# The front of a deformable-convolution stage: weights as 128 rows, positions as a tenth tap, tap 8 selected from the parts, another first item in the ring of PSUM banks

## The chip, the core and the metric

The kernel runs on one core of one Trainium2 chip. The metric is the device time of one execution in microseconds (us). PE is the matmul engine (TensorE), ACT evaluates functions and evicts PSUM (ScalarE), DVE is VectorE, POOL is GpSimd, SP issues most DMAs (SyncE). Engines run their own instruction streams and wait for each other on semaphores. Matmuls here are float32, and each one appears in the trace as two passes.

## The reference

Five stages follow each other on x of shape (8, 32, 16, 16); the change lies in the first, and the other four (a convolution with Fourier attention, Nystrom attention, two mixtures of layers with data-dependent routing) stay as they are.

```python
x = x + deform(groupnorm(x), w_off, b_off, w_dcn)     # groups of one channel
# deform: KK = 9 taps, 18 offset channels (dy, dx per tap)
offset = conv3x3(x, w_off) + b_off
y  = row - 1 + ky + dy ;  xc = col - 1 + kx + dx       # sampling position
sampled[c, k, n] = bilinear(x[c], y[k, n], xc[k, n])   # zero outside
out[o, n] = sum_{c, k} sampled[c, k, n] * w_dcn[o, c, k]
```

## The kernel before

The data lies as 128 partitions: 4 images (`bi`) times 32 channels, with two groups (`g`) of 256 pixels in the free dimension, so one tile is 128x512. DVE normalizes x into `xnp` (with a border) and `xn` (semaphore `xn`); ACT gives the square root in between (`var`, `std`).

The offset convolution is 36 matmuls of 32x32 (line 539): per image one bank `ps[0..3]`, and in the bank the four 32-row column groups take taps k % 4. The sampling positions (row, column, tap shift and bias, from the four rows of `lineb`) are one matmul into `ps[4]` (line 532) ahead of it. The four banks are evicted to four tiles, the `parts4`: two by ACT (line 1181), two by DVE (line 1464). A matmul with `eye32` adds up the column groups of each part in `ps[4]` (line 565), and ACT evicts the sum as `offC` (line 1194).

A position enters as a hat function of its distance to each grid line. Matmuls with 0/1 weights select the rows of `offC` for each tap: line 572 selects tap 8 of all images into `ps[2]` (`sel8_w`), line 577 taps 0 to 3 of one image each into `ps[3..6]`. ACT takes the absolute distance (line 1189, `distance`), and DVE cuts it to the hat (line 1472, `hat`). Then comes the ring: "items" of four matmuls into four of the banks 0 to 6 in rotation. `expand` (line 632) spreads a hat to the pixel grid for one image, `expand8` (line 640) does so for tap 8 of the four images, and both are squared on the way out: three banks by ACT (`squares`, line 1209), one copied by DVE (line 1500) and squared by POOL (line 427). Weight items (`half_of_weights`, line 550) multiply `xn` with the taps' weights, and ACT and DVE evict them (lines 1185, 1468). The products of the two (line 649) add up in bank 7, which a matmul with zeros opens (line 677). `bank_free` writes the waits for each item's banks by hand, `FILL_ACT`, `FILL_DVE`, `ACT_FILL` and `DVE_FILL` count what each engine has evicted before item 0, and the order of items on each engine is written out.

The loads: SP issues x, `lineb`, two blocks of constants (`cstb`), `parb` and `rowb`; ACT issues the early columns of the weights `w32b` in two DMAs, each broadcast from 32 rows to four copies. SP then waits for both and issues the late loads. `par_in` is one semaphore for `lineb`, `parb` and `rowb`.

Of the kernel before, what the change touches and what calls it, by code (L numbers as in the profile page):

```python
# [20 lines left out]
ACT = mybir.ActivationFunctionType  # L21
# [18 lines left out]
SMALL = 16 * 3  # L40
LATE = 16 * 10

# [3 lines left out]
for _n, _k in (("off", KK * C), ("dcn", KK * C), ("conv", KK * CH), ("qkv", 3 * P), ("gate", EXP), ("ln", 2),  # L46
               ("v", LAYERS * LHEADS * C), ("q", LAYERS * LHEADS * C)):
    W32[_n] = (_at, _at + _k)
    _at += _k
W32_COLS = _at  # L50
W32_OFF, W32_EARLY = W32["off"][1], W32["conv"][1]
# [4 lines left out]
for _n, _k in (("mask4", BI), ("eye32", C), ("negq", 1), ("sel8", 8), ("spread", PT * P), ("gather", PT * 32),  # L56
               ("ident", P), ("flip", P), ("mask8", HEADS),
               ("rep16", P), ("mask16", P), ("swap", P), ("dft", PT * 2 * N)):
    CST[_n] = (_at, _at + _k)
    _at += _k  # L60
CST_COLS = _at
CST_EARLY, CST_MID = CST["sel8"][1], CST["gather"][1]


PAR = ("bn_g", "bn_b", "bn_m", "bn_v", "cg2_w", "cg2_b", "cg1_w", "cg1_b", "cgbn_g", "cgbn_b", "cgbn_m",
       "cgbn_v", "tau", "gate_b")
ROWS = {"b_out": (0, C)}
ROW_COLS = C


LINES = P + BG * N
# [7 lines left out]
    "x_in", "cst_in", "mid_in", "w32_in", "taps_in", "par_in", "late_in",  # L79
# [24 lines left out]
FILL_ACT = {"part": 1, "weights": 3, "sum": 5, "far": 6}  # L104
FILL_DVE = {"part": 1, "weights": 3, "more": 5}
ACT_FILL, DVE_FILL = 10, 8
GROUPS = {1: (1, 2, 3, 4), 2: (8, 9, 11, 12), 3: (14, 15, 16, 17), 4: (18, 19, 20, 21)}
ITEM = {1: (0, 0, 0), 2: (0, 0, 1), 3: (0, 0, 2), 4: (0, 0, 3), 8: (0, 1, 0), 9: (0, 1, 1), 11: (0, 1, 2),
        12: (0, 1, 3), 14: (1, 0, 0), 15: (1, 0, 1), 16: (1, 0, 2), 17: (1, 0, 3), 18: (1, 1, 0), 19: (1, 1, 1),
        20: (1, 1, 2), 21: (1, 1, 3)}  # L110
SQUARED = (0, 1, 2, 3, 4, 7, 8, 9, 11, 12, 14, 15, 16, 17, 18, 19, 20, 21)
FREED = {8: 1, 9: 2, 11: 3, 12: 4, 14: 6, 15: 5, 16: 7, 17: 8, 18: 9, 19: 10, 20: 11, 21: 12}
G_ITEM, SEL_ITEM, GC_ITEM = {5: 0, 6: 1}, 10, 13
ALL_DCN = 18
EX_COUNT = {0: 1, 1: 2, 2: 3, 3: 4, 4: 5, 7: 6, 8: 7, 9: 8, 11: 9, 12: 10, 13: 11, 14: 13, 15: 14, 16: 15, 17: 16,
            18: 17, 19: 18, 20: 19, 21: 20}
# [24 lines left out]
def build(nc, x, cst, w32, par, rows, lines, toep, w_out, moe_w1, moe_w2, moe_b2, am, fm, keys, rec_a, rec_b, out):  # L141
    ctx = ExitStack()
    with ctx:
# [9 lines left out]
        parb = sb("parb", len(PAR))  # L153
        rowb = sb("rowb", ROW_COLS)
# [16 lines left out]
        def row_(n):  # L171
            return rowb[:, ROWS[n][0]:ROWS[n][1]]

# [13 lines left out]
        lineb = sb("lineb", LINES, parts=4)  # L187
# [31 lines left out]
        sel_w, sel8_w = outf, gatef[:, 0:P]  # L219
# [111 lines left out]
        def home(item, j):  # L331


            first = {0: 0, 1: 4, 2: 8, 3: 12, 4: 16, 7: 20, 8: 0, 14: 20}
            if item in first:
                return room[first[item] + j]
            column = {9: (1, 0), 11: (1, 1), 12: (1, 2), 15: (1, 3), 16: (2, 0), 17: (2, 1), 18: (2, 2), 19: (2, 3),
                      20: (3, 0), 21: (3, 1)}[item]
# [6 lines left out]
        def _(sp):  # L345
            sp.dma_start(xC.rearrange("p (g n) -> p g n", g=BG),
                         x.rearrange("(g b) c n -> (b c) g n", g=BG)).then_inc(S["x_in"], 16)
            sp.dma_start(lineb, lines).then_inc(S["par_in"], 16)
            sp.dma_start(cstb[:, 0:CST_EARLY], cst[:, 0:CST_EARLY]).then_inc(S["cst_in"], 16)
            sp.dma_start(cstb[:, CST_EARLY:CST_MID], cst[:, CST_EARLY:CST_MID]).then_inc(S["mid_in"], 16)  # L350
            sp.dma_start(parb, par.unsqueeze(0).to_broadcast([B, CH, len(PAR)])).then_inc(S["par_in"], 16)
            sp.dma_start(rowb, rows.partition_broadcast(P)).then_inc(S["par_in"], 16)
            sp.wait_ge(S["w32_in"], 16)
            sp.wait_ge(S["taps_in"], 16)
            sp.dma_start(cstb[:, CST_MID:CST_COLS], cst[:, CST_MID:CST_COLS]).then_inc(S["late_in"], 16)
            sp.dma_start(w32b[:, W32_EARLY:W32_COLS], w32[:, W32_EARLY:W32_COLS].unsqueeze(0)
# [1622 lines left out]
```

## Time and profile before

| | |
|---|---|
| median of 3 runs | 344.14 us (341.44 to 345.53) |
| the profiled execution | 342.19 us, span 340.2 us |
| mean granted clock of TensorE | 0.948 |
| busy PE, DVE, ACT, POOL | 84%, 48%, 43%, 16% of the span |
| first piece of the product stretch | 35.91 us |
| end of the stage's matmuls | 75.34 us |

Busy shares are means over stages with different limits: the first 36 us are the part to read closely. The span goes from the first to the last instruction; the time includes what lies around it.

### The profile page before, as it was taken

What the parts mean: (1) busy time and instruction counts of PE and PEld (TensorE: products, weight loads), DVE (VectorE), ACT (ScalarE), POOL (GpSimd) and SP (SyncE); (2) the same over time, 40 slices, a digit from 0 to 9 for tenths busy, and PEclk for the clock granted to TensorE, in tenths of its full rate; (3) what the DMA queues carried; (4) which work ended last, traced back from release to release, by engine and by line L of the source; (5) the groups of instructions that cost most, each with busy time, mean ns of one, the idle gap of its engine ahead of it and who ended that gap; (6) DMA issues with size and microseconds to landing.
All of it is one profiled execution on the core that took longest, in us unless ns stands there. A gap on an engine that the chain in (4) does not pass through costs nothing.

```text
span 340.2 us, 5837 instructions
## 1 busy us (share of the span) xinstructions
PE 286.2 (84%) x1954; PEld 168.8 (50%) x1954; DVE 163.4 (48%) x423; ACT 145.5 (43%) x329; POOL 54.1 (16%) x61
## 2 busy tenths in 40 slices
PE   5989999999888999989988789778976787588873
PEld 1333333357335798979953465666422442125521
DVE  3152335823767559787656544113413763126730
ACT  1156786733525634646423301120141692225940
POOL 3104826521006000160000002330000000000001
PEclk9698999999999899999998959999999999879999
DMA  3864200000000000000000000000000000000000
GB/s 100 204 122 100 78 0 4 2 2 0 2 0 1 0 2 0 3 1 0 2 0 0 2 0 0 0 0 3 2 19 17 0 0 0 17 17 0 0 0 31
DMA packets 4193, 6.20 MB, mean 18 GB/s; under 512 B 1318, under 2 KB 3750, under 8 KB 4013
## 3 DMA queue, kind: packets, MB, share of 16 engines
q1 hardware_dynamic: 3910, 5.58, 7.2%
q10 hardware_dynamic: 264, 0.37, 0.3%
q8 instruction: 12, 0.20, 0.3%
q14 instruction: 7, 0.06, 0.1%
HBM read 5.69 MB, written 0.26 MB: 17 GB/s over the span
## 4 chain that ended last, share of the span: by engine, by line
PE 59%; DVE 16%; ACT 7%; issue 7%; DMA 6%; SPq 2%; DVEq 1%; ACTq 0%
PE ps L649 6%; PE ps L632 6%; PE ps L517 5%; DMA recB<-rec_b 4%; PE ps L883 4%; PE ps L889 3%; PE ps L1018 2%; PE ps L871 2%; ACT arena L1383 2%; DMA rowb<-rows 2%; DVE rmax L1845 2%; PE ps L1130 2%; PE ps L539 1%; PE ps L1010 1%; PE ps L823 1%
## 5 line engine op out<-in xcount | busy, mean ns | idle before, releaser
L517 PE MATMUL ps<-xC,cstb 128*128 128x512 f32 x102 | 50.6, 640 | 0.0
L517 PEld LDWEIGHTS ps<-xC,cstb 128*128 128x128 f32 x102 | 20.2, 207 | 25.3 <-issue 25.0
L632 PE MATMUL ps<-arena,cstb 32*128 32x512 f32 x128 | 22.2, 652 | 0.6 <-ACT arena L1189 0.6
L1209 ACT ACTIVATE bds<-ps 128x512 f32<-128x512 f32 x32 | 17.2, 599 | 7.4 <-PE ps L632 6.1
L486 POOL TENSOR_TENSOR arena<-w32b,cstb 128x1024 f32<-128x1024 f32 x4 | 7.6, 1894 | 64.7 <-PEq L1004 50.8
L495 POOL TENSOR_TENSOR ln_a<-tC,hC 128x512 f32<-128x512 f32 x1 | 1.3, 1263 | 104.1 <-DVE hC L1880 104.1
L649 PE MATMUL ps<-bds,arena 128*32 128x256 f32 x160 | 17.4, 384 | 0.0
L883 PE MATMUL ps<-arena 128*128 128x160 f32 x96 | 15.3, 307 | 2.3 <-issue 1.2
L1383 ACT ACTIVATE arena<-ps,rmax 128x256 f32<-128x256 f32 x32 | 14.8, 470 | 5.2 <-DVE rmax L1845 5.2
L883 PEld LDWEIGHTS ps<-arena 128*128 128x128 f32 x96 | 13.3, 190 | 3.4 <-DVE arena L1708 1.9
L1400 ACT ACTIVATE arena<-ps,w2c 128x512 f32<-128x512 f32 x16 | 9.7, 688 | 11.2 <-PE ps L1130 11.2
L1100 PE MATMUL ps<-cstb,arena 128*128 128x128 f32 x64 | 10.5, 286 | 4.3 <-DVE arena L1853 4.2
L1137 PE MATMUL ps<-arena,w2c 128*32 128x512 f32 x32 | 12.0, 718 | 1.8 <-ACT arena L1400 1.8
L1164 ACT ACTIVATE small<-small 128x16 f32<-128x16 f32 x5 | 1.1, 216 | 28.1 <-DVE small L1427 27.2
L649 PE MATMUL ps<-arena 128*32 128x256 f32 x128 | 12.9, 382 | 0.0
L1845 DVE TENSOR_REDUCE rmax<-ps 128x2 f32<-128x512 f32 x16 | 10.8, 684 | 4.2 <-PE ps L1089 4.2
L632 PEld LDWEIGHTS ps<-arena,cstb 32*128 32x128 f32 x128 | 7.0, 193 | 11.4 <-issue 6.0
L427 POOL TENSOR_TENSOR bds<-bds 128x512 f32<-128x512 f32 x8 | 9.1, 1133 | 21.6 <-DVE bds L1500 21.6
L1100 PEld LDWEIGHTS ps<-cstb,arena 128*128 128x128 f32 x64 | 6.7, 140 | 10.7 <-DVE arena L1853 10.7
L889 PE MATMUL ps<-arena,bds 128*128 128x64 f32 x96 | 11.4, 272 | 0.0
L1096 PE MATMUL ps<-cstb 128*128 128x256 f32 x32 | 9.8, 387 | 1.9 <-ACT arena L1383 1.9
L1853 DVE TENSOR_TENSOR arena<-arena,rsum 128x512 f32<-128x512 f32 x16 | 11.1, 692 | 0.6
(418 smaller groups left out, 602.0 us busy)
## 6 DMA issues: line engine op xcount, KB each, us to landing
toepb<-toep SPq DMA_DIRECT2D x1, 1536.0 KB
w32b<-w SPq DMA_DIRECT2D x1, 1225.0 KB
cstb<-cst SPq DMA_DIRECT2D x1, 836.0 KB
recA<-rec_a SPq DMA_DIRECT2D x4, 128.5 KB
w1b<-moe_w SPq DMA_DIRECT2D x1, 264.0 KB
xC<-x SPq DMA_DIRECT2D x1, 256.0 KB, 2.7
w2b<-moe_w SPq DMA_DIRECT2D x1, 256.0 KB
out<-ln_a SPq DMA_DIRECT2D x1, 256.0 KB, 2.2
```

What stands on the lines that cost most here:

```text
L517: mm(ps[bank], ident if lhs is None else lhs, xC if rhs is None else rhs, start=True, stop=True)
L632: last = mm(bank_of(item, j), spread[rows, half, :], hats[1 + 4 * kg + bi][rows, :], start=True, stop=True)
L649: return mm(ps[7][32 * bi:32 * bi + 32, g * N:g * N + N], weights, moving[:, g * N:g * N + N], start=False, stop=stop, skip_group_check=True)
L883: last = mm(ps[q][:, 160 * j:160 * j + 160], bdY[:, b, :], YV[:, b, :], start=True, stop=True)
L889: last = mm(ps[q][:, 320 + 64 * j:384 + 64 * j], bdY2[:, 2 * q + j, :, :], pG[:, 2 * q:2 * q + 2, :], start=True, stop=True)
L1096: mm(ps[a][:, 0:N], ident, cstb[:, 0:N], start=True, stop=True)
L1100: last = tr(ps[a][:, (u * PT + t) * P:(u * PT + t + 1) * P], pr[:, a * 512 + t * N + u * P:a * 512 + t * N + u * P + P], ident)
L1137: last = mm(ps[1][32 * bi:32 * bi + 32, :], w2c[:, 0:C], f1[:, 512 * bi:512 * bi + 512], start=True, stop=True)
L1209: af(home(item, j), bank_of(item, j), ACT.Square).then_inc(S["bank_act"], 1)
L1383: last = af(pr[:, b * 512 + t * N:b * 512 + t * N + N], ps[b][:, t * N:t * N + N], ACT.Exp, bias=rmax[:, 2 * b + t:2 * b + t + 1], accum_o ...
L1845: v_.tensor_reduce(rmax[:, 2 * b:2 * b + 2], arr3(ps[b], N), AX.X, ALU.max, negate=True).then_inc(S["sc_max"], 1)
L1853: tt_(pb3, pb3, r.unsqueeze(2).to_broadcast([P, 2, N]), ALU.mult).then_inc(S["sc_norm"], 1)
```

## The change

- `w32` is stored with 128 rows, its four copies written out. Its early columns now hold the offset weights, then the weights and lines of the positions (`base`, `lines`), and SP loads them in one DMA right behind x. ACT loads the taps' columns, and waits for x before it issues that. `parb` and `rowb` become columns of the constants; `lineb`, `parb` and `rowb` are no longer loaded by themselves.
- The positions become a tenth tap: four matmuls beside tap 8, into the column group of taps 1 and 5. PE warms up with one matmul, the one that opens bank 7 with zeros, and one more.
- Tap 8 is selected from the four parts instead of from `offC`.
- The ring begins with tap 8's spread in banks 0 to 3; DVE copies three of these banks and POOL squares them, ACT squares the fourth. The weights of half 0, group 1 become item 1; the old items 1 to 21 become 2 to 22 in the same banks.

```diff
@@ loads @@
-            sp.dma_start(lineb, lines).then_inc(S["par_in"], 16)
+            sp.dma_start(w32b[:, 0:W32_OFF], w32[:, 0:W32_OFF]).then_inc(S["w32_in"], 16)
...
-            sp.dma_start(parb, par.unsqueeze(0).to_broadcast([B, CH, len(PAR)])).then_inc(S["par_in"], 16)
-            sp.dma_start(rowb, rows.partition_broadcast(P)).then_inc(S["par_in"], 16)
-            sp.wait_ge(S["w32_in"], 16)
             sp.wait_ge(S["taps_in"], 16)
...
-            act.dma_start(w32b[:, 0:W32_OFF], w32[:, 0:W32_OFF].unsqueeze(0)
-                          .to_broadcast([BI, C, W32_OFF])).then_inc(S["w32_in"], 16)
-            act.dma_start(w32b[:, W32_OFF:W32_EARLY], w32[:, W32_OFF:W32_EARLY].unsqueeze(0)
-                          .to_broadcast([BI, C, W32_EARLY - W32_OFF])).then_inc(S["taps_in"], 16)
+            act.wait_ge(S["x_in"], 16)
+            act.dma_start(w32b[:, W32_OFF:W32_EARLY], w32[:, W32_OFF:W32_EARLY]).then_inc(S["taps_in"], 16)
@@ PE @@
+                    if k == KK - 1:
+                        mm(ps[bi][32:64, :], w32_("base")[rows, :],
+                           w32_("lines")[rows, :].unsqueeze(1).to_broadcast([32, BG, N]), start=False, stop=True,
+                           skip_group_check=True)
...
-            mm(ps[2], sel8_w, offC, start=True, stop=True
-               ).then_inc(S["sel_mm"], 1)
+            for bi in range(BI):
+                last = mm(ps[2][32 * bi:32 * bi + 32, :], sel8_w, parts4[bi], start=True, stop=True,
+                          skip_group_check=True)
+            last.then_inc(S["sel_mm"], 1)
@@ DVE @@
+            for bi in range(BI):
+                dve.wait_ge(S["bank_act"], FAR + bi)
+                hat(1 + bi)
+                if bi < 3:
+                    dve.wait_ge(S["ex_mm"], EX_COUNT[0])
+                    v_.tensor_copy(home(0, bi), ps[bi]).then_inc(S["bank_dve"], 1)
```

On PE at the program's start (`T` is the warm-up's data, L517 before and L524 after; L551 is the convolution after, L548 the positions), before:

```order
L517 MATMUL ps<-T 128x512 [waits pool_zero]
L517 MATMUL ps<-T 128x512 x2
L532 MATMUL ps<-lineb 128x512 [waits par_in]
L539 MATMUL ps<-arena,w32b 32x512 [waits w32_in,xn]
L539 MATMUL ps<-arena,w32b 32x512 x35
```

and after:

```order
L524 MATMUL ps<-T 128x512 [waits pool_zero]
L539 MATMUL ps<-T,zeros 128x512 [waits pool_zero]
L524 MATMUL ps<-T 128x512
L551 MATMUL ps<-arena,w32b 32x512 [waits xn,w32_in]
L551 MATMUL ps<-arena,w32b 32x512 x31
L548 MATMUL ps<-w32b 32x512
L551 MATMUL ps<-arena,w32b 32x512
```

The wait for `par_in` and its matmul are gone, the clearing of bank 7 stands in the warm-up, and the positions alternate with the last four matmuls of the convolution (the pair L548, L551 comes four times).

On PE from the sum of the parts on (`outf` and `gatef` hold the select weights, `cstb` the spread's), before:

```order
L565 MATMUL ps<-tC,cstb 32x512
L572 MATMUL ps<-arena,gatef 128x512 [waits pool_bd,bank_act]
L577 MATMUL ps<-arena,outf 128x512 [waits bank_act]
L577 MATMUL ps<-arena,outf 128x512 x3
L550 MATMUL ps<-w32b,arena 128x288 [waits bank_dve] x2
L550 MATMUL ps<-w32b,arena 128x288 [waits bank_act] x2
L640 MATMUL ps<-arena,cstb 128x512 [waits bank_act,hat,mid_in]
L640 MATMUL ps<-arena,cstb 128x512 [waits bank_act] x2
L640 MATMUL ps<-arena,cstb 128x512 [waits bank_dve]
L677 MATMUL ps<-arena,zeros 128x512 [waits pool_zero]
L632 MATMUL ps<-arena,cstb 128x512 [waits bank_dve,hat]
```

and after:

```order
L584 MATMUL ps<-ln_a,gatef 32x512 [waits pool_bd]
L584 MATMUL ps<-ln_b,gatef 32x512
L584 MATMUL ps<-lnC,gatef 32x512
L584 MATMUL ps<-tC,gatef 32x512
L590 MATMUL ps<-arena,outf 128x512 [waits bank_dve,bank_act]
L590 MATMUL ps<-arena,outf 128x512 x3
L648 MATMUL ps<-arena,cstb 128x512 [waits bank_dve,hat,mid_in]
L648 MATMUL ps<-arena,cstb 128x512 [waits bank_dve]
L648 MATMUL ps<-arena,cstb 128x512 [waits bank_act] x2
L562 MATMUL ps<-w32b,arena 128x288 [waits bank_act] x3
L562 MATMUL ps<-w32b,arena 128x288 [waits bank_dve]
L640 MATMUL ps<-arena,cstb 128x512 [waits bank_dve,hat]
```

Tap 8's select no longer waits for ACT's `offC`, the four weight matmuls have moved behind tap 8's spread (L640 before, L648 after), and no clearing matmul stands before the first item of taps 0 to 3 (L632 before, L640 after).

On DVE from the parts to the ring (`lnC` and `tC` are parts, 128x288 the weights, `bds` evicted items), before:

```order
L1464 COPY tC<-ps 128x512 [waits off_mm]
L1468 TENSOR_SCALAR arena<-ps 128x288 [waits g_mm] x2
L1472 TENSOR_SCALAR arena<-arena 128x512 [waits bank_act] x2
L1468 TENSOR_SCALAR arena<-ps 128x288 [waits g_mm] x2
L1472 TENSOR_SCALAR arena<-arena 128x512 [waits bank_act] x2
L1468 TENSOR_SCALAR arena<-ps 128x288 [waits g_mm] x2
L1472 TENSOR_SCALAR arena<-arena 128x512 [waits bank_act]
L1500 COPY bds<-ps 128x512 [waits ex_mm] x3
```

and after:

```order
L1473 COPY tC<-ps 128x512 [waits off_mm]
L1477 TENSOR_SCALAR arena<-ps 128x288 [waits g_mm] x3
L1481 TENSOR_SCALAR arena<-arena 128x512 [waits bank_act] x2
L1495 COPY bds<-ps 128x512 [waits ex_mm]
L1481 TENSOR_SCALAR arena<-arena 128x512 [waits bank_act]
L1495 COPY bds<-ps 128x512 [waits ex_mm]
L1481 TENSOR_SCALAR arena<-arena 128x512 [waits bank_act]
L1495 COPY bds<-ps 128x512 [waits ex_mm]
L1481 TENSOR_SCALAR arena<-arena 128x512 [waits bank_act]
```

Four weight evictions between the hats are gone, and three copies of tap 8's spread (L1495) stand there instead.

## Rows read from the trace of the kernel before

**Rows 1.** Chain of waits in order of time, 0 to 37 us: start, us, what.

```profile
3.37 5.65 DMA rowb<-rows
...
9.06 2.07 PE ps L532 x2
11.13 4.76 PE ps L539 x72
...
17.46 1.04 PE ps L565 x8
...
18.53 0.61 ACT arena L1194
...
20.30 1.11 PE ps L577 x8
21.41 0.68 ACT arena L1189
```

**Rows 2.** The same chain, 35 to 78 us: first and last product pieces.

```profile
35.91 1.00 PE ps L649 x16
...
68.30 7.04 PE ps L649 x128
```

**Rows 3.** Timeline, 0 to 9 us: start us, us, engine, line, operation, out<-in.

```profile
0.74 1.18 ACTq L1170 DMA_DIRECT2D w32b<-w  x1
...
1.31 4.32 PE L517 MATMUL ps<-T 128*128 128x512 f32 x6 [1.31 <-POOL T L401]
...
1.94 0.55 ACTq L1172 DMA_DIRECT2D w32b<-w  x1
...
2.52 1.28 ACT L1175 ACT_TABLE_LOAD   x1 [2.52 <-issue]
...
3.50 0.89 DVE L1446 BATCH_NORM_STATS2 scr<-xC 128x6 f32<-128x256 f32 x2 [3.50 <-DMA xC<-x]
...
5.06 0.20 ACT L1175 ACTIVATE small<-small 128x2 f32<-128x2 f32 x1 [1.26 <-DVE small L1449]
...
5.50 0.74 DVE L1455 TENSOR_SCALAR arena<-xC,scr,small 128x256 f32<-128x256 f32 x2
```

**Rows 4.** Windows: stretch, busy time by engine, last granted clock, DMA share, GB/s.

```profile
2.50:3.00 0.50, 0.50 (x2) 0.17 (x1) 0.00 (x0) 0.48 (x1) 0.44 (x2) 1.00 1.01 340
...
6.50:7.00 0.50, 0.00 (x0) 0.00 (x0) 0.46 (x2) 0.00 (x0) 0.29 (x1) 1.00 0.27 96
...
7.50:8.00 0.50, 0.00 (x0) 0.00 (x0) 0.00 (x0) 0.00 (x0) 0.00 (x0) 0.73 0.27 81
...
14.00:15.00 1.00, 1.00 (x36) 0.42 (x7) 0.00 (x0) 0.00 (x0) 0.00 (x0) 0.72 1.11 181
...
24.00:25.00 1.00, 1.00 (x6) 0.17 (x5) 1.00 (x3) 0.00 (x0) 0.00 (x0) 0.90 0.29 69
...
28.00:29.00 1.00, 1.00 (x14) 0.49 (x6) 0.21 (x1) 0.21 (x1) 0.00 (x0) 0.90 0.30 88
```

**Rows 5.** Timeline of the ring's head, 20 to 31 us.

```profile
21.06 0.43 DVE L1472 TENSOR_SCALAR arena<-arena 128x512 f32<-128x512 f32 x1 [3.10 <-ACT arena L1189]
...
24.99 2.08 PE L677 MATMUL ps<-arena,zeros 128*128 128x512 f32 x2
...
25.10 0.69 DVE L1500 COPY bds<-ps 128x512 f32<-128x512 f32 x1
25.87 1.04 POOL L427 TENSOR_TENSOR bds<-bds 128x512 f32<-128x512 f32 x1 [15.22 <-DVE bds L1500]
...
28.79 1.57 ACT L1209 ACTIVATE bds<-ps 128x512 f32<-128x512 f32 x3 [2.11 <-PE ps L632]
...
30.60 1.57 ACT L1209 ACTIVATE bds<-ps 128x512 f32<-128x512 f32 x3 [0.23 <-PE ps L632]
```

**Rows 6.** Timeline of weight loads (PEld) in the convolution: starts of two passes.

```profile
11.92 0.17 PEld L539 LDWEIGHTS ps<-arena,w32b 32*32 32x32 f32 x1 [0.58 <-issue]
12.78 0.17 PEld L539 LDWEIGHTS ps<-arena,w32b 32*32 32x32 f32 x1 [0.68 <-issue]
```

More of the change, by code:

```diff
@@ L39 @@
 NONE = 4096
-SMALL = 16 * 3
 LATE = 16 * 10
+PAR = ("bn_g", "bn_b", "bn_m", "bn_v", "cg2_w", "cg2_b", "cg1_w", "cg1_b", "cgbn_g", "cgbn_b", "cgbn_m",
+       "cgbn_v", "tau", "gate_b")
 W32 = {}
 _at = 0
-for _n, _k in (("off", KK * C), ("dcn", KK * C), ("conv", KK * CH), ("qkv", 3 * P), ("gate", EXP), ("ln", 2),
+for _n, _k in (("off", KK * C), ("base", C), ("lines", N), ("dcn", KK * C), ("conv", KK * CH), ("qkv", 3 * P), ("gate", EXP), ("ln", 2),
                ("v", LAYERS * LHEADS * C), ("q", LAYERS * LHEADS * C)):
@@ L50 @@
 W32_COLS = _at
-W32_OFF, W32_EARLY = W32["off"][1], W32["conv"][1]
+W32_OFF, W32_EARLY = W32["lines"][1], W32["conv"][1]
 CST = {}
 _at = 0
-for _n, _k in (("mask4", BI), ("eye32", C), ("negq", 1), ("sel8", 8), ("spread", PT * P), ("gather", PT * 32),
+for _n, _k in (("mask4", BI), ("eye32", C), ("negq", 1), ("par", len(PAR)), ("b_out", C), ("spread", PT * P), ("gather", PT * 32),
                ("ident", P), ("flip", P), ("mask8", HEADS),
@@ L434, in _ @@
                 nc.gpsimd.tensor_tensor(hats2[n], hats[n], hats[n], ALU.mult).then_inc(S["hat_sq"], 1)
-            for item in SQUARED[5:]:
+            for item in SQUARED[4:]:
                 square_copy(item)
@@ L1209, in squares @@
                     af(home(item, j), bank_of(item, j), ACT.Square).then_inc(S["bank_act"], 1)
-            for item in range(22):
+            act.wait_ge(S["ex_mm"], EX_COUNT[0])
+            af(home(0, 3), bank_of(0, 3), ACT.Square).then_inc(S["bank_act"], 1)
+            for item in range(1, 23):
                 if item in G_ITEM:
+                    half, g, n = G_ITEM[item]
                     for bi in range(3):
-                        weight_half(1, G_ITEM[item] * BI + bi, 9 + 4 * G_ITEM[item] + bi, bank_of(item, bi)
-                                    ).then_inc(S["bank_act"], 1)
+                        weight_half(half, g * BI + bi, n + bi, bank_of(item, bi)).then_inc(S["bank_act"], 1)
                 elif item == SEL_ITEM:
@@ L1895, in constants @@
     put("ident", np.eye(P))
+    put("par", np.tile(par, (B, 1)))
+    put("b_out", np.tile(b_out, (P, 1)))
     put("flip", np.eye(P)[::-1])
```

269 lines of the change are left out of this document (128 added, 141 removed).

## The prediction

> **What bounds the kernel now.** I read the chain of waits first, since only time on it can be won. Until 35.9 us it is a mixture: a DMA, PE pieces with gaps, single ACT evictions [rows 1]. From 35.91 us to the end of the stage at 75.34 us it is PE work at the full granted clock, piece after piece [rows 2]. The diff leaves that stretch and all that follows as they are (ring item i+1 now uses the banks that item i used). So I ask one question: how much earlier does the 35.91 piece start? The reader should see three things in the front. The offset convolution (L539) starts at 11.13 although its input is scaled at 6.24, because PE first waits for the last of three small loads until 9.02 and then makes the positions in 2.07 us (L532) [rows 1, 3]. The convolution then runs at half clock (1.2 GHz): PE finished its warm-up at 5.63, the granted clock fell during 7.5 to 8 us and rose again only at about 14.6 [rows 3, 4]. And the head of the ring takes 7.4 us from the first of the four distances (21.41) to the first full set of squares after tap 8's (28.79), 2.08 us of it a matmul that clears bank 7 [rows 1, 5].
>
> **The start of the convolution.** The three small loads and L532 go; PE now waits for the scaled input and the early weights. The early weights are 295 KB (2304 B in each of 128 rows), second in SP's queue behind x. Data of x is through at about 3.0 us, and DVE starts on x at 3.50 [rows 3, 4]. Bounds for moving 295 KB: 0.9 us at the 340 GB/s of 2.5 to 3 us, 3.1 us at the 96 GB/s of 6.5 to 7 us [rows 4]; with 0.5 us to the semaphore they are there between 4.4 and 6.6 us. I take the early end, nearer to x, a load of the same 128 rows. In the 96 GB/s stretch the DMA share is 0.27, about 4 of 16 engines, while the old weight loads, broadcast as four copies, were the large ones left [rows 4]. The Trainium skill ("DMA: Bandwidth & Descriptors", the section on why a DMA increments its semaphore by 16) says that the slowest dimension sets how many engines a DMA uses, so that four copies use four; this trace agrees with its 0.27, and by that rule the 128 rows would go at the high rate (0.9 us), while a load of four copies would cost 3.1 us.
>
> Neither bound reaches the other condition. ACT now waits for x, issues one load and only then loads its table (1.28 us; before, it did so at 2.52, hidden behind x) [rows 3]. An issue after a wait isn't in the trace; the two ACT issues took 1.18 and 0.55 us, and I take 0.55, as the new one has a plain 2-D source. The root then starts at 3.50 + 0.55 + 0.04 + 1.28 = 5.37 instead of 5.06, and from the root to the end of the scaling it is 6.24 - 5.06 = 1.18 us [rows 3]. Start at 6.6 us (7.2 with the longer issue; 6.3 if the issue is so short that the root starts as before). Against 11.13 that is **4.5 us**. Behind ACT's wait stand only its load and the root; the load, issued at about 4 us, is first needed at 9 us.
>
> **Its length.** The 36 matmuls come in three groups (taps 0-3, 4-7, 8) of two passes each, 0.86 us apart at half clock [rows 6], so 0.43 at full clock; with the 0.18 us by which two full-clock passes exceed 0.86 (L565: 1.04 us) [rows 1] it is 2.8 us instead of 4.76. The tenth tap goes into a column group that tap 8 leaves free, beside it; sixteen such tiles ran side by side in the earlier groups. It costs nothing, or at worst one group, 0.9 us. The warm-up is still six passes (one of the three matmuls now clears bank 7), so it ends at about 5.63 and PE stands still for 1.0 us, not 3.4. I take the full clock: **2.0 us**, end at 9.4.
>
> **Tap 8 from the parts.** Before, the sum (L565) ends at 18.50, ACT evicts it (0.61), and L572 runs until the selects at 20.30 [rows 1]. Now tap 8's four matmuls follow L565 directly, 0.87 us of passes, with that eviction beside them. From the convolution's end the selects ended at 21.41 - 15.89 = 5.5 us; now 1.57 + 0.87 + 1.04 + 1.11 = 4.6. **0.9 us**, distance 1 at 14.0.
>
> **The ring's head.** Weights of tile group g=1 leave the fill and become ring item 1; the clearing matmul is gone from here. Tap 8's spread needs banks 0 to 3; bank 3 is free with distance 1 (0.68), then 1.2 us until the evictions start (as in the ring, where the next squares start 30.60 - 28.79 us after the last, of which the first eviction, that frees the bank, takes some 0.6) [rows 1, 5]. What is late next is DVE. It now evicts three banks of tap 8, alternating with hats: copy 0.69, hat 0.43, copy, hat, copy = 2.9 us [rows 5]. The next spread (item 2) waits for the last copy, and 1.2 us later the squares start: 0.7 + 1.2 + 2.9 + 1.2 = 6.0 us instead of 7.4, **1.4 us**. Item 1 (weights) lies inside this time: PE waits for distance 4 and the first copy, both before the second copy ends, and the one ACT eviction on which item 2 waits comes about 0.9 us before the third copy ends. GpSimd has three squares of tap 8 where it had one (1.04 us each against copies 1.12 apart [rows 5]), so it ends about 1 us behind the last copy, well ahead of tap 8's product. From the first squares on, order and counts match before: the 7.1 us from 28.79 to 35.91 stay.
>
> **What the clock takes back.** Without the clearing matmul, PE has only item 1's weights to do between the spread of tap 8 and item 2, some 3 us. Even with more work there the trace fell to half clock at about 24.8 and rose at about 28.2 [rows 4]. At half clock item 2 costs 0.5 us more (27.07 to 28.79 is 1.72 against 1.2) [rows 5], the next period about 0.8 and tap 8's product 0.5. I count **1.8 us** lost; the bounds are 0 and 3.4 (as much again).
>
> **Sum.** 4.5 + 2.0 + 0.9 + 1.4 - 1.8 = 7.0 us. The profiled execution took 342.19 us (span 340.2), so its own time would be 335.2. The median of the runs shown is 1.95 us above it, and they spread over 4.1 us; halfway I forecast **336.0 us**.
>
> **Rivals.**
> - The clock holds through the ring's head: no 1.8, gain 8.8 us, 334.2. For it: the full clock held from 14.6 to 24.8 us although PE waited for ACT's eviction from 18.5 on and for others behind it [rows 1, 4].
> - The convolution runs at half clock: 6 x 0.86 + 0.18 = 5.3 us, 2.5 more, gain 4.5, 338.5 (337.5 if the fall comes midway). For it: in the trace the clock fell at about 7.7, and the convolution then is only about 1 us old; against it, PE stands still for 1 us, not for 2 before that moment. The Trainium skill ("TensorE: Matmul & The Clock Gate", Part 1) calls the gate's watch free-running, not reset by a kernel's start; by that rule the fall's moment isn't tied to when PE stopped and can differ from run to run. No row here decides it.
> - The wait only moves: weights, taps or ACT's table arrive late, at the 96 GB/s of a crowded DMA (x, early weights, two blocks of constants and taps are 978 KB, which then take 10 us). The convolution starts cold at about 9: 2.4 and 2.0 us of the gain go, 2.6 remain, 340.4. Against it, the three loads of tiny rows are gone.
> - The ring's head gives nothing, or tap 8 doesn't come forward: 1.4 and 0.9 off, 4.7 remain, 338.3. It decides if DVE's copies reach 4.3 us instead of 2.9.
> - Slower: the granted clock stays at half from the convolution on. The fill until the first product piece then eats the 7 us (2.5 in the convolution, half a microsecond to one in each of some six pieces of the fill), and from there each microsecond of dense full-clock PE work costs another. It decides from about 4.4 us of such work on (347.6 us); ten pieces of 1 us make 353. Against it, the clock rose within 5.6 us of PE's restart at 9.06 and once more at 28.2, each time under work [rows 1, 4].
>
> **How the numbers follow.** Forecast 0.40, clock holds 0.22, cold convolution 0.20, wait only moves 0.08, ring gives nothing 0.07, slower 0.03. A time within 1% (3.4 us) of 344.14 is about what a measurement here cannot tell from no change. Faster by more: the first, second, third and fifth, with a third of the fourth, less a little for run spread, 0.90; within 1%: 0.07; slower: 0.03. The range goes from the second case with the shorter issue and run spread (334.2 - 2.2) to the cold convolution with run spread (338.5 + 1.5): 332 to 340.
>
> **What would show it.** L551, the convolution, starts at 6.2 to 7.2 us, released by DVE's scaling (right) or by the weights' DMA (first term wrong); its passes lie 0.43 apart at a granted clock of 1.00. ACT's table load starts after 3.9 us. The first set of squares starts at 19 to 22 us, and the matmul before it was released by DVE's third copy. The stretch from the first product of group 1 to the end of the stage stays 39.4 us. I am wrong if the first squares start after 25 us, or if time is lost behind 75 us, where I expect none.

## The result, and the profile after

| | median of the runs | before, beside it | ratio, 95% interval |
|---|---|---|---|
| changed kernel, first measurement | 333.52 us (4 runs) | 343.39 us (4) | 0.9644 [0.9554, 0.9733] |
| the same kernel again | 333.07 (6) | 341.0 (17) | 0.976 [0.9705, 0.9814] |
| again2 | 337.92 (6) | 341.3 (11) | 0.9865 [0.979, 0.994] |
| again3 | 337.91 (6) | 342.24 (17) | 0.9763 [0.9689, 0.9836] |
| again5 | 333.45 (6) | 341.22 (11) | 0.9745 [0.9688, 0.9802] |
| kernel before against itself (null1) | 341.35 (12) | 342.24 (17) | 0.9958 [0.9924, 0.9992] |

A ratio leaves out runs more than 1.5% above the fastest of their kernel (337.72 and 336.03 us in the first measurement), so it is not always the quotient of the medians. The change is faster, as forecast. Against the median of 344.14 us the forecast of 336.0 is a ratio of 0.976 and the range is 0.965 to 0.988. The first measured ratio lies below the forecast by more than its interval, and just under the range (0.9644 x 344.14 = 331.9 us). It rests on two runs of the changed kernel, 331.01 and 330.3 us; the medians of all four give 333.52 / 343.39 = 0.971, which is inside the range. The four repeats lie inside it too. Counting every run, 29 runs of the changed kernel have a mean of 335.55 us, 68 of the kernel before (those beside the four repeats, and null1's twelve) 341.83: 6.3 us apart, 0.982. So the first number was not the size of the change. The sections below ask where the 6.3 us come from and why single measurements scatter from 0.964 to 0.987.

The first profile after took 337.72 us (span 335.5, mean granted clock 0.939). Its chain of waits, in order of time (start us, us, what):

```profile
6.66 2.52 PE ps L551 x64
9.92 1.68 PE ps L562 x8
...
14.78 1.65 PE ps L648 x7
16.45 0.69 DVE bds L1495
...
18.22 4.05 PE ps L640 x16
...
27.61 1.00 PE ps L658 x16
...
41.70 3.51 PE ps L715 x16
...
61.59 7.04 PE ps L658 x128
```

The convolution starts at 6.66 and is done at 9.92 (before: 11.13 and 15.89 [rows 1]). Group 1's first product piece starts at 27.61 instead of 35.91 [rows 2], 8.3 us earlier. The stage ends at 61.59 + 7.04 = 68.63 instead of 75.34, 6.7 us earlier: 1.6 us are lost in between, in L715, which took 3.51 us at half clock (granted clock 0.51 from 41.7 to 45.2 us) where the same piece took 1.88 before. Behind the stage another 2.0 are lost, since the span is only 4.7 shorter. In the timeline of the same kernel, the start of the front:

```profile
3.62 0.39 ACTq L1183 DMA_DIRECT2D w32b<-w  x1
...
4.04 1.28 ACT L1185 ACT_TABLE_LOAD   x1 [4.04 <-DMA xC<-x]
...
5.34 0.20 ACT L1185 ACTIVATE small<-small 128x2 f32<-128x2 f32 x1
...
5.77 0.74 DVE L1464 TENSOR_SCALAR arena<-xC,scr,small 128x256 f32<-128x256 f32 x2
...
6.66 0.72 PE L551 MATMUL ps<-arena,w32b 32*32 32x512 f32 x16 [1.07 <-DVE arena L1464]
```

PE is released by DVE's scaling and no longer by a DMA: the early weights were there before, 3.0 us after their issue at 1.25. In two of the repeats below (again, again5) PE's own warm-up comes last instead, at 6.80 us; the start is the same within 0.15 us. The timeline of the ring's head in the same kernel:

```profile
14.55 2.42 ACT L1199 ACTIVATE arena<-ps,cstb 128x512 f32<-128x512 f32 x4 [0.33 <-PE ps L590]
...
17.39 0.68 DVE L1495 COPY bds<-ps 128x512 f32<-128x512 f32 x1
...
18.57 0.68 DVE L1495 COPY bds<-ps 128x512 f32<-128x512 f32 x1
...
20.50 1.57 ACT L1216 ACTIVATE bds<-ps 128x512 f32<-128x512 f32 x3 [2.13 <-PE ps L640]
...
22.30 1.57 ACT L1216 ACTIVATE bds<-ps 128x512 f32<-128x512 f32 x3 [0.23 <-PE ps L640]
```

From distance 1 (14.55) to the first full squares (20.50) it is 5.95 us, where it was 7.38 [rows 5]. Windows of the same kernel show the granted clock (third number from the end; then DMA share and GB/s):

```profile
3.00:3.50 0.50, 0.50 (x2) 0.32 (x1) 0.00 (x0) 0.00 (x0) 0.09 (x1) 1.00 1.04 397
14.00:19.00 5.00, 4.48 (x26) 1.97 (x18) 3.40 (x7) 4.03 (x9) 1.78 (x2) 1.00 1.01 356
19.00:24.00 5.00, 5.00 (x39) 1.89 (x39) 2.58 (x5) 3.15 (x6) 3.69 (x4) 1.00 0.04 9
24.00:29.30 5.30, 5.23 (x48) 2.04 (x48) 1.84 (x3) 4.06 (x9) 3.47 (x5) 1.00 0.01 3
```

In this execution the clock stays at 1.00 from the convolution to 41.8 us. The DMA moves 397 GB/s in all, at a share of 1.04, where 96 GB/s at a share of 0.27 stood while the copies of before were on their way [rows 4].

### The profile page after: what moved, and what is told of

It reads as the page before. It is cut to its first block, busy times and chain, and to the rows that moved or that the text cites. A ratio compares the mean times of both kernels' runs of the same rounds, so it can differ in the third digit from the quotient of the medians.

```text
span 335.5 us, 5855 instructions
## 1 busy us (share of the span) xinstructions
PE 286.6 (85%) x1964; PEld 169.3 (50%) x1964; DVE 165.0 (49%) x423; ACT 145.1 (43%) x329; POOL 56.6 (17%) x63
## 4 chain that ended last, share of the span: by engine, by line
PE 59%; DVE 17%; ACT 8%; issue 7%; DMA 5%; SPq 2%; DVEq 1%; ACTq 0%
PE ps L658 6%; PE ps L640 6%; PE ps L524 5%; DMA recB<-rec_b 4%; PE ps L895 4%; PE ps L901 3%; PE ps L1030 2%; PE ps L883 2%; ACT arena L1392 2%; PE ps L1142 2%; DVE rmax L1853 2%; PE ps L1022 1%; PE ps L835 1%; PE ps L756 1%; PE ps L1120 1%
## 5 line engine op out<-in xcount | busy, mean ns | idle before, releaser
L524 PE MATMUL ps<-xC,cstb 128*128 128x512 f32 x102 | 51.0, 644 | 0.0
L524 PEld LDWEIGHTS ps<-xC,cstb 128*128 128x128 f32 x102 | 20.4, 209 | 27.0 <-issue 26.7
L640 PE MATMUL ps<-arena,cstb 32*128 32x512 f32 x128 | 22.6, 633 | 0.9 <-ACT arena L1199 0.6
L1216 ACT ACTIVATE bds<-ps 128x512 f32<-128x512 f32 x29 | 15.6, 598 | 6.1 <-PE ps L640 6.1
L1149 PE MATMUL ps<-arena,w2c 128*32 128x512 f32 x32 | 13.5, 941 | 1.8 <-ACT arena L1409 1.8
L640 PEld LDWEIGHTS ps<-arena,cstb 32*128 32x128 f32 x128 | 7.2, 183 | 10.9 <-issue 3.9
L901 PEld LDWEIGHTS ps<-arena,bds 128*128 128x128 f32 x96 | 11.2, 192 | 0.0
```

Of the source, the lines that this page charges most:

```text
L524: mm(ps[bank], ident if lhs is None else lhs, xC if rhs is None else rhs, start=True, stop=True)
L640: last = mm(bank_of(item, j), spread[rows, half, :], hats[1 + 4 * kg + bi][rows, :], start=True, stop=True)
L901: last = mm(ps[q][:, 320 + 64 * j:384 + 64 * j], bdY2[:, 2 * q + j, :, :], pG[:, 2 * q:2 * q + 2, :], start=True, stop=True)
L1149: last = mm(ps[1][32 * bi:32 * bi + 32, :], w2c[:, 0:C], f1[:, 512 * bi:512 * bi + 512], start=True, stop=True)
L1216: af(home(item, j), bank_of(item, j), ACT.Square).then_inc(S["bank_act"], 1)
```

## The experiments

Two questions stood first. Which of the four parts carries the gain: the start, the tenth tap, tap 8 from the parts, or the new order of the ring? And is the front's granted clock a thing of the order of work, or of the execution? Each expectation names its theories by letters of its own.

### The same kernel again (again, again2, again3, again4, again5)

No edit.

> The changed kernel unchanged, timed once more beside before, to see how far its runs spread and whether time goes with the mean granted clock. Theory A (the front alone, 8.3 us earlier; the rest of the difference is the granted clock behind the stage, which falls differently from run to run): both kernels spread over 4 to 8 us, in each kernel longer runs have the lower mean clock, and the mean of all runs differs by 8 to 10 us. Theory B (something behind the stage also got faster): the shortest runs of both kernels differ by 11 us or more, and so do the longest, at equal clock.

> The changed kernel unchanged, timed beside the same runs of before. Theory A: the gain is about 8 us, ratio 0.973 to 0.980, and the first comparison's 0.964 came from few runs with a high granted clock. Theory B (12 us are real): ratio 0.968 or lower.

> The changed kernel, unchanged, a fourth time, against the kernel before on the same chip. Of the 44 timed runs so far the means are 341.4 us before (28 runs) and 335.0 after (16), 6.3 us apart. Theory A (the change is worth what the front shows, 8.3 us where the clock stays up, less what the granted clock takes back in some executions): 0.975 to 0.985, about 335. Theory B (the first ratio, 0.964, is the size of the change, and the later ones were pulled down by the chip): 0.960 to 0.970. In the trace: first full squares at 20.4 to 20.9 us and group 1's piece of product at 27.6 to 28.1 us where the clock holds, 21.5 to 22 and 31.5 to 32 us where it falls at 19 to 29 us.

> The changed kernel, unchanged, a fifth look. Theory A (the front's half clock falls at random in about one execution in ten, one of ten profiles with the early start so far): the front at full clock, piece of product at 27.6 to 28.1 us. Theory B (it is as common as one in three, one of the three profiles of this very kernel): as likely as not piece of product at 31.5 to 32 us.

> The changed kernel, unchanged, beside the run before it. Theory A: within 0.007 of that run's ratio. Theory B: slower than it by about 0.01, and half clock at 19 to 29 us in the trace (two of the five profiles so far), with group 1's piece of product at 31.5 to 32 us.

The ratios stand in the table; again4 (one run) took 339.84 us. In again the means lie 7.8 us apart, a little under the 8 to 10 of its theory A. First product piece of group 1 in the six profiles of this kernel: 27.61, 27.94, 27.74 (again4), 27.84 (again5), but 31.59 in again2 and 31.59 in again3. The chain of waits of again2:

```profile
18.29 5.95 PE ps L640 x16
24.24 1.86 PE ps L658 x16
26.10 4.07 PE ps L640 x16
...
31.59 1.00 PE ps L658 x16
```

and its windows:

```profile
14.00:19.00 5.00, 4.48 (x26) 1.97 (x18) 3.33 (x7) 4.10 (x9) 1.71 (x2) 1.00 1.04 355
19.00:24.00 5.00, 5.00 (x15) 1.76 (x14) 1.96 (x4) 1.57 (x3) 2.84 (x3) 0.50 0.08 21
24.00:29.30 5.30, 5.30 (x32) 2.26 (x32) 1.38 (x2) 2.69 (x6) 1.38 (x2) 0.50 0.00 0
```

From the convolution to 18.3 us again2 does the same as the first profile, within 0.1 us. Then the clock falls at 19.0 and rises at 29.3. Item 2 takes 5.95 instead of 4.05, tap 8's product 1.86 instead of 1.00, and the loss at the first product piece is 31.59 - 27.78 = 3.8 us (27.78 is the mean of the other four). This is the take-back that the prediction placed here, at twice its price, in two executions of six; in the other four it is nothing. How often it comes is poorly known: the four variants below that keep the new ring and start as early (clear_late, copies_first, tap_order, table_early) don't show it, one profile each.

One thing did differ ahead of the convolution: the last two passes of the warm-up, here in the first profile, again2 and again.

```profile
4.57 1.02 PE L524 MATMUL ps<-T 128*128 128x512 f32 x2
...
4.89 1.27 PE L524 MATMUL ps<-T 128*128 128x512 f32 x2
...
4.89 1.92 PE L524 MATMUL ps<-T 128*128 128x512 f32 x2
```

In again4 they took 1.02 us, in again5 1.91, in again3 1.31. So the clock had risen ahead of these passes in two executions that kept it later, rose behind them in two more that kept it, and rose during them in the two that lost it. That is a pointer, no proof: clear_late below, where the clock also rose during these passes (its warm-up ends at 6.51 us, against 6.19 in again3 and 6.80 in again), kept it.

Behind the front the clock differs as well: again4 has full clock in the whole front and still took 339.84, with a half-clock stretch from 202.5 to 226.4 us that no other profile has.

### The kernel before again (null1, null2)

No edit.

> The kernel before, unchanged, against itself: a measurement of nothing, and a second look at its front. Theory A (the half clock in the front belongs to the order of work: the shifted product of warm-up, wait and convolution brings the clock down at about 7.7 us in every execution): the convolution's first matmul again at 11.1 us and some 4.8 us long, the ring's head (distance 1 to the first full squares) again 7.4 us, first full squares at 28 to 29.5 us, group 1's first piece of product at 35 to 36.5 us. Theory B (the half clock there belongs to the execution, as in the changed kernel, where one of three profiles has 10.2 us of it in the ring's head and stage and two have none): start again at 11.1 us, but in some profile a convolution of about 2.9 us, a ring's head of 5.8 us, squares at 25 to 26 us and the piece of product at 31 to 32 us; then 2 to 4 us of the gain measured from one pair of profiles belong to the execution and not to the change. The ratio: 1.00, and how far it lies from that says what the three ratios of the changed kernel (0.964, 0.976, 0.987) can differ by for nothing.

> The kernel before, unchanged, a third look at its front. Theory A: half clock at 7 to 15 us and again at 24 to 29 us, convolution 4.8 us, squares at 28 to 29.5 us. Theory B: one or both of these stretches missing or elsewhere, squares at 25 to 28 us.

Null1 took 341.35 us against itself at 342.24, 0.9958: an interval that leaves out 1 for no change at all. Null2 took 340.9. Windows of null1:

```profile
10.00:14.00 4.00, 4.00 (x70) 1.70 (x72) 0.00 (x0) 0.00 (x0) 0.65 (x1) 0.57 0.92 298
...
24.00:29.30 5.30, 5.30 (x20) 1.69 (x18) 1.40 (x3) 3.02 (x6) 1.71 (x2) 0.68 0.25 65
```

and its timeline:

```profile
9.06 1.12 PE L532 MATMUL ps<-lineb 4*128 4x512 f32 x2 [2.26 <-DMA rowb<-rows]
...
10.11 4.70 PE L539 MATMUL ps<-arena,w32b 32*32 32x512 f32 x72
...
27.86 1.57 ACT L1209 ACTIVATE bds<-ps 128x512 f32<-128x512 f32 x3 [2.22 <-PE ps L632]
```

Theory A's two stretches of half clock are there, but the convolution starts a microsecond earlier than it expected. The kernel before loses the clock in its front in all three profiles: in the convolution (from 10.44 to 13.84 us here, from 10.28 to 13.70 in null2, from 7.72 to 14.56 in the profile of the prediction) and again at about 24 to 28 us. The profile that I predicted from had the longest first stretch: its L532 ran at half clock (2.07 us [rows 1]), here it takes 1.12. So its first product piece came late, at 35.91 against 34.97 and 34.77; the mean of the three is 35.22.

### The start alone (start_only)

The kernel before, with the early weights as 128 rows, the new loads and the tenth tap. Tap 8's select, the ring's order and the place of the clearing matmul stay as before. The edit, against the kernel before:

```diff
+            sp.dma_start(w32b[:, 0:W32_OFF], w32[:, 0:W32_OFF]).then_inc(S["w32_in"], 16)
...
-            pe.wait_ge(S["par_in"], SMALL)
-            mm(ps[4], lineb[:, 0:P], lineb[:, P:LINES], start=True, stop=False, skip_group_check=True)
...
+                        mm(ps[bi][32:64, :], w32_("base")[rows, :],
```

> The kernel before with the loads, the tenth tap and nothing else of the change (selection from the sum, old ring, clearing matmul before item 1 of the ring, warm-up of three matmuls). Theory A: convolution starts at 6.6 us and ends at 9.9 at full clock, 6.0 us sooner than before; the ring's first full squares start 12.2 to 12.9 us behind that (22.1 to 22.8), so 6.0 to 6.7 us of the gain are here and 1.6 to 2.3 in the rest of the change. Rival (the ring's order is what brings the gain, the start only moves the wait): squares start after 25 us.

Median 334.03 us (6 runs), ratio 0.9817 [0.9761, 0.9874]: most of the gain. The timeline of the ring's head:

```profile
15.34 2.42 ACT L1179 ACTIVATE arena<-ps,cstb 128x512 f32<-128x512 f32 x4 [0.36 <-PE ps L569]
...
18.88 1.12 PE L669 MATMUL ps<-arena,zeros 128*128 128x512 f32 x2
...
21.14 1.57 ACT L1199 ACTIVATE bds<-ps 128x512 f32<-128x512 f32 x3 [0.57 <-PE ps L624]
```

With the old order and the clearing matmul in it, the head takes 21.14 - 15.34 = 5.80 us at full clock, and the squares come a microsecond earlier than theory A expected. Before took 7.38 in the profile shown and 7.45 in null1, where L677 took 1.97 to 2.08 at half clock. So the ring's head was not long because of its order; it was long because of its clock. What the 128 rows alone carry, and what the dropped small loads and L532, no run separates.

### Start and select, old ring (start_select, start_select5, start_select6)

Against the changed kernel, the ring's tables and POOL's three squares go back to the kernel before, and the clearing matmul with them:

```diff
-GROUPS = {1: (2, 3, 4, 5), 2: (9, 10, 12, 13), 3: (15, 16, 17, 18), 4: (19, 20, 21, 22)}
+GROUPS = {1: (1, 2, 3, 4), 2: (8, 9, 11, 12), 3: (14, 15, 16, 17), 4: (18, 19, 20, 21)}
...
-            for j in range(3):
-                pool.wait_ge(S["bank_dve"], DVE_FILL + 1 + j)
-                v = home(0, j)
-                nc.gpsimd.tensor_tensor(v, v, v, ALU.mult).then_inc(S["sq_pool"], 1)
```

> The kernel with the loads, the tenth tap and tap 8 selected from the parts, but the old ring (weights of group 1 inside the fill, clearing matmul before the ring's item 1). Theory C (the new order of the ring's head is worth nothing: what looked like its gain was the half clock in the trace of before): from the convolution's end to the first full squares 10.3 to 10.7 us, about 1 less than with the loads and the tenth tap alone (11.4) and no more than in the changed kernel (10.6). Rival, the step of the prediction (the new head is 1.4 us shorter): 12.0 us.

> The kernel with the loads, the tenth tap and tap 8's selection, old ring, now timed. Theory C (the new ring's head is worth nothing): same time as the changed kernel beside it, 332 to 335 us, ratio to before 0.973 to 0.980. Rival (the new head is worth its 1.4 us): 1.4 us slower than the changed kernel, ratio higher by 0.004. Half a per cent is about what five rounds can tell.

> The kernel before with the early weights, the tenth tap and tap 8 from the parts, but the old order of the ring and the old place of the clearing matmul, timed again beside the changed kernel on one chip. On the one chip that ran both, it took 0.976 and the changed kernel 0.987. Theory A (that was the granted clock of those executions; the two orders cost the same): the two ratios within 0.007 of each other, both near 0.98. Theory B (the old order keeps the clock up behind tap 8 more often, since a clearing matmul of 128 rows by 512 columns stands in the head of the ring): again about 0.976 here against 0.98 to 0.987, and no half clock at 19 to 29 us in the trace, product of group 1 at 27.4 to 27.9 us.

One run took 329.82 us; timed, 333.21 (6 runs), ratio 0.9759 [0.9705, 0.9814], on the chip on which again2 took 0.9865; timed once more, 332.66 (6), 0.9738 [0.9697, 0.9779], beside again5's 0.9745. The timeline of start_select:

```profile
14.63 2.42 ACT L1181 ACTIVATE arena<-ps,cstb 128x512 f32<-128x512 f32 x4 [0.33 <-PE ps L571]
...
18.17 1.12 PE L671 MATMUL ps<-arena,zeros 128*128 128x512 f32 x2
...
20.43 1.57 ACT L1201 ACTIVATE bds<-ps 128x512 f32<-128x512 f32 x3 [0.57 <-PE ps L626]
```

The convolution's end is the start of the next piece in the chain of waits, here of start_only and of start_select:

```profile
9.73 1.68 PE ps L542 x8
...
10.01 1.68 PE ps L543 x8
```

From the convolution's end to the squares it is 10.42 us (20.43 - 10.01); in start_only 11.41 (21.14 - 9.73), in the changed kernel 10.58 (20.50 - 9.92). Tap 8 from the parts is worth 1.0 us, and the new order of the ring, with the clearing matmul moved, is worth nothing at full clock; its head is 5.95 us long against 5.80 in the old order. This version is as fast as the changed kernel with the simpler ring. Whether it is faster (13 runs have a mean of 332.5 us against 335.55) stays open: none of its three profiles has half clock in the front, against two of six, and in the second pair the two were level. Group 1's first product piece starts at 27.26 to 27.55 us in the three, against 27.61 to 27.94 in the four profiles of the changed kernel at full clock.

### The clearing matmul put back (clear_late)

```diff
-            pe.wait_ge(S["pool_zero"], 3)
-            mm(ps[7], zeros, T, start=True, stop=False, skip_group_check=True)
-            keep_busy(1, T[:, 0:P], T, bank=6)
+            keep_busy(2, T[:, 0:P], T, bank=6)
...
+            pe.wait_ge(S["pool_zero"], 3)
+            mm(ps[7], zeros, xn, start=True, stop=False, skip_group_check=True)
```

> The changed kernel with the matmul that clears bank 7 back in the ring's head, right after tap 8's spread (the warm-up has three plain matmuls). Theory A (DVE's three copies are what is late there, PE has room): its 1.1 us lie in PE's wait for the copies; first full squares move by 0 to 0.4 us. Rival (the clearing matmul was the price of the old head): squares move by 1.1 us or more, 21.6 or later.

332.13 us (one run). In its timeline the matmul is back in the head:

```profile
16.31 1.13 PE L688 MATMUL ps<-arena,zeros 128*128 128x512 f32 x2
...
18.55 0.68 DVE L1495 COPY bds<-ps 128x512 f32<-128x512 f32 x1
...
20.47 1.58 ACT L1216 ACTIVATE bds<-ps 128x512 f32<-128x512 f32 x3 [1.30 <-PE ps L638]
```

The squares start 10.57 us after the convolution's end, as in the changed kernel (10.58): 1.13 us of PE work lies beside DVE's copies and costs nothing. What ends last there is the third copy.

### DVE's copies ahead of the hats (copies_first)

```diff
-            for bi in range(BI):
+            dve.wait_ge(S["bank_act"], FAR)
+            hat(1)
+            for bi in range(3):
+                dve.wait_ge(S["ex_mm"], EX_COUNT[0])
+                v_.tensor_copy(home(0, bi), ps[bi]).then_inc(S["bank_dve"], 1)
+            for bi in range(1, BI):
...
```

> The changed kernel with DVE's three copies of tap 8's spread ahead of hats 2 to 4 instead of alternating with them. Theory E (the ring's head waits for DVE's third copy): the copies end 0.7 to 0.8 us sooner, and the first full squares start 9.8 to 9.9 us after the convolution's end instead of 10.6. Rival (another wait stands right behind, the weights of item 1 or their eviction): under 0.3 us.

334.99 us (one run). Its timeline:

```profile
16.73 1.89 DVE L1494 COPY bds<-ps 128x512 f32<-128x512 f32 x3 [0.75 <-PE ps L648]
...
19.86 1.57 ACT L1216 ACTIVATE bds<-ps 128x512 f32<-128x512 f32 x3 [1.22 <-PE ps L640]
...
22.93 1.57 ACT L1216 ACTIVATE bds<-ps 128x512 f32<-128x512 f32 x3 [1.49 <-PE ps L640]
```

The first squares come 9.66 us after the convolution's end instead of 10.58, 0.9 earlier, so DVE's third copy was the late one, as forecast. The next set comes 3.07 us behind instead of 1.80: the hats that were put off are late now, and with them the eviction of weights behind them (L1477, for which PE waits until 21.7 us). The first product piece is at 28.22, 18.0 us after the convolution's end against 17.7. The gain is given back one item later.

### The positions behind tap 8 (tap_order)

```diff
-                    if k == KK - 1:
-                        mm(ps[bi][32:64, :], w32_("base")[rows, :],
...
+            for bi in range(BI):
+                rows = slice(32 * bi, 32 * bi + 32)
+                mm(ps[bi][32:64, :], w32_("base")[rows, :],
```

> The changed kernel with the four matmuls of the positions behind tap 8's four instead of alternating with them. Theory D (the tenth tap costs 0.4 us only because two matmuls of one row group stand next to each other and their weight loads wait): the convolution takes 2.8 to 2.9 us instead of 3.26. Rival (eight tiles in the last group cost that in any order): 3.2 to 3.3 us.

336.47 us (one run), with the convolution from 6.69 to 9.96: 3.27 us, against 3.26. The order of the eight matmuls doesn't matter: either is some 0.45 us, about one pass of 0.43, above the 2.8 reckoned for nine taps (no run has nine taps at full clock throughout). Why eight tiles don't run side by side there, when sixteen did in the earlier groups, is open.

### The early weights late (weights_late, weights_late2)

```diff
-            sp.dma_start(w32b[:, 0:W32_OFF], w32[:, 0:W32_OFF]).then_inc(S["w32_in"], 16)
...
+            sp.dma_start(w32b[:, 0:W32_OFF], w32[:, 0:W32_OFF]).then_inc(S["w32_in"], 16)
```

It stands behind the wait for the taps now.

> The changed kernel with the early weights issued only after the taps have landed, so that PE stands still about 3 us after the warm-up instead of 1. If the clock is a cost of its own (theory A): convolution starts at about 8.6 us at half clock and takes about 5 us instead of 3.3, so its end moves by 3.7 us, about 1.9 of it for the later start; the first full squares start at about 24 us. Rival (the clock does not matter for the convolution, loads of weights limit it): length stays 3.3 us and everything moves by 1.9 us only.

> The changed kernel with late early weights, profiled once more, because its timed runs were longer than its first profile. Theory A (in most executions the convolution then runs at half clock): start at 9.0 us, length 5 us instead of 3.3, first full squares at 24.5 to 27 us. Rival (something behind the stage is longer): convolution at full clock and squares at 22.8 us as in the first profile, with a long time all the same.

Median 340.99 us (10 runs), ratio 0.994 [0.989, 0.999]; the second execution profiled (weights_late2) took 343.06. The timeline of the second:

```profile
9.03 4.16 PE L551 MATMUL ps<-arena,w32b 32*32 32x512 f32 x65 [2.68 <-DMA w32b<-w]
...
22.18 5.95 PE L640 MATMUL ps<-arena,cstb 32*128 32x512 f32 x16 [0.27 <-DVE bds L1495]
...
25.40 1.57 ACT L1216 ACTIVATE bds<-ps 128x512 f32<-128x512 f32 x3 [3.09 <-PE ps L640]
```

In the first profile (334.81 us) the convolution started at 8.96 and ran 3.28 us at full clock, and the product piece came at 29.93, 2.15 later than in the changed kernel, which is the later start and no more. In the second the convolution was at half clock and so was the ring's head; the piece came at 35.43. The first is the rival's forecast, the second theory A's: the two profiles of one kernel lie 5.5 us apart in the front. The later load costs 2.2 us by the wait itself and, in one profile of two, as much again and more by the clock; the timed runs, with a mean of 340.3 over both, lie 4.8 us above the changed kernel's.

### No warm-up but the clearing matmul (no_warm)

```diff
-            keep_busy(1, T[:, 0:P], T, bank=6)
...
-            keep_busy(1, T[:, 0:P], T, bank=6)
```

> The changed kernel without the two warm-up matmuls (only the one that clears bank 7 stands ahead of the convolution), so that the convolution begins at half clock. Theory A (the clock is a term of its own): start at 6.7 us, passes 0.86 us apart, length 4.5 to 5.5 us instead of 3.3, and the first full squares 1.5 to 3 us later, 22 to 23.5 us. Rival (evictions and DVE hide it): squares move by under 0.5 us.

341.52 us (one run). Its chain of waits:

```profile
6.66 4.34 PE ps L549 x65
11.66 1.74 PE ps L560 x8
...
33.32 1.00 PE ps L656 x16
```

The convolution starts at the same 6.66 and takes 5.0 us, with passes 0.85 apart; the clock is at half again from 20.8 to 31.0. The product piece is 5.5 us later than 27.78. The convolution alone is 1.7 us longer (5.0 against 3.26), which prices the rival in which it runs at half clock, put at 2.5; the other 3.8 come with the second stretch of half clock.

### The table loaded ahead of x (table_early)

```diff
-            act.wait_ge(S["x_in"], 16)
-            act.dma_start(w32b[:, W32_OFF:W32_EARLY], w32[:, W32_OFF:W32_EARLY]).then_inc(S["taps_in"], 16)
...
+            act.dma_start(w32b[:, W32_OFF:W32_EARLY], w32[:, W32_OFF:W32_EARLY]).then_inc(S["taps_in"], 16)
```

The first square root, which brings the table, now stands ahead of the load of the taps.

> The changed kernel with ACT's load of the taps behind the square root, so that the table is loaded while x is still on its way. Theory F (ACT's wait for x puts the table load on the path, 0.3 us): the square root starts 0.3 us sooner against x's landing and the convolution starts 6.3 to 6.4 us, unless the warm-up ends later. Rival (taps come late then): the weight matmuls behind the convolution wait for the load.

333.54 us (one run). The timeline of ACT:

```profile
0.73 1.28 ACT L1183 ACT_TABLE_LOAD   x1 [0.73 <-PEq L1980]
5.25 0.20 ACT L1183 ACTIVATE small<-small 128x2 f32<-128x2 f32 x1 [3.23 <-DVE small L1457]
```

The root starts at 5.25 instead of 5.34, since DVE's statistics are the other condition: the table behind the wait costs 0.1 us. The convolution starts at 6.73, no earlier; here the warm-up itself ends only then.

## Why the prediction was right, and where it failed

**The start** (4.5 us): right, 11.13 - 6.66 = 4.47, released by DVE as named. The early end of the 4.4 to 6.6 us was the right one; the table's load started at 4.04 behind an issue of 0.39 us, where I took 0.55. With the early weights as 128 rows the DMA share was 1.04, with the four copies of before 0.27. The Trainium skill ("DMA: Bandwidth & Descriptors", the section on why a DMA increments its semaphore by 16) says that the slowest dimension sets the number of engines; the two shares agree. Against null1 and null2 the term is 3.5 and 3.3, because L532 took 1.12 there and not 2.07.

**Its length** (2.0 us): mis-sized, 4.76 - 3.26 = 1.50. "It costs nothing, or at worst one group": it cost about one pass, half a group: seven passes of 0.43 and 0.18 make 3.2. Full clock in the convolution was right in the six profiles of the changed kernel (3.26 to 3.45 us; in again, the longest, the clock rose only during the first passes).

**Tap 8 from the parts** (0.9): right. From the convolution's end to distance 1 it was 5.52 and is 4.63; start_only against start_select gives 1.0.

**The ring's head** (1.4): right in size, 7.38 - 5.95 = 1.43, and DVE's third copy is what is late, but the cause was wrong. I credited the new order and the clearing matmul. Start_select and clear_late show that both are worth nothing at full clock; the 1.4 to 1.6 us were the half clock of the old head, which all three profiles of before have.

**What the clock takes back** (1.8): this is the step that failed. I charged one price to every execution, "I count 1.8 us lost". Measured, it is 0 in four profiles and 3.8 in two, with the same instructions ahead of it and item 2 starting between 18.2 and 18.6 us in all six. So the reason that I gave, too little work for PE between tap 8's spread and item 2, doesn't decide it: that work was the same in all six. The first profile had none, so its front gained 8.3, which is the sum without this term (8.8) less the tenth tap's pass. The rival "the clock holds" described that execution.

**Sum and spread.** The prediction took one profile of before as the kernel's own time. Its front was the slowest of three: 35.91 against a mean of 35.22. With that, the product piece gains 35.22 - 27.78 = 7.4 us where the clock holds, less 3.8 in two of six, 6.2 on average; the timed means lie 6.3 apart. That the two agree is support, not proof, for the clock behind the stage differs too. That the forecast sum of 7.0 lies so near is partly luck: between the means of the profiles (three of before, six after) the start gains 3.7 us and not 4.5, the convolution's length 1.4 and not 2.0, while the clock takes back 1.3 on average and not 1.8. (Halfway between 335.2 and the median's 1.95 above it is 336.2, not 336.0.) Over the 127 timed runs of before, the changed kernel, start_only, start_select and weights_late, a fit with one level for each kernel and one common slope gives 0.32 us for each us at half clock (taken as 2 x (1 - mean clock) x span). At equal half clock the changed kernel lies 4.8 us below before, start_select 5.6, start_only 4.4, weights_late 2.2, each good to 0.4 to 0.8 us; and the changed kernel spends 33.9 us at half clock on average against 38.5, worth 1.5.

**The range** missed the first ratio at its low end, by 0.1 us, and here the term that was too small is the run spread. I gave it and the shorter issue 2.2 us together, but the runs of the changed kernel alone go from 330 to 344.5 us. The first ratio rests on 330.3 and 331.0 us, 7.1 below the profiled run, whose front had already kept its clock; at the slope above, their mean clock (0.964 and 0.968 against 0.939) is worth 6.0 of that. They have no profile, so where in them the clock was better isn't shown. The median of before beside them lies 1 to 2.4 us above its later ones. "Time lost behind 75 us" was named as a sign of error, and 2.0 us were lost there in that profile; again5, whose front is the same within 0.3 us, has a span of 327.8 us against 335.5, and at that slope its clock (0.974 against 0.939) is worth all of it. It is the execution's clock, not the change. Why the clock holds or falls in a given execution stays open.

The Trainium skill ("TensorE: Matmul & The Clock Gate", Part 1) calls the gate's watch free-running; that the fall came at 7.72, 10.44 and 10.28 us in three executions of before, and at 19.0 or not at all in six of the changed kernel, agrees.

## What to carry to other kernels

Take the small loads and their wait from in front of the first matmuls: the start (with the tenth tap) and the select carried the whole gain here, and the reordered ring carried none. Before a stretch is called long because of its order, look at the granted clock in it, in more than one profile of the same kernel; a clock's take-back belongs in the range with its own chance, not in the sum as a mean. And when an early wait is removed, ask what the next item waits for: copies_first won 0.9 us and gave it back 3 us later.

## What was not expected of the hardware

- Two executions of one program, equal to 0.1 us from the convolution to 18.3 us, differ from 19.0 to 29.3 us by a granted clock of 1.00 or 0.50, and by 3.8 us at the next product piece. Their warm-up differed: its last two passes took 1.02 and 1.27 us.
- Four 32x32 tiles of another operand, put beside four in the last group of a convolution, cost about a whole pass (0.43 us) over the 2.8 us reckoned without them, in either order.
- An ACT issue of a DMA right behind a wait took 0.39 us; the 288 KB of early weights as 128 rows arrived while the DMA moved 363 to 397 GB/s in all, where 96 stood while four broadcast copies were on their way [rows 4].
- The kernel before, measured against itself, gave 0.9958 [0.9924, 0.9992].
